# Four graph stages on one core: weight scatters placed after all gathers instead of between them

## What is computed

```python
agg = segment_sum(h[src], dst, N) / max(deg, 1); h = agg @ Wl.T + bl + h @ Wr.T      # stages 0, 1
agg = segment_sum(h[src] * norm, dst, N); h = relu(agg + b) @ W_lin + b_lin          # stages 2, 3, 4
for l in range(3):                                                                   # stages 5 to 13
    for k in (1, 2, 3):
        x = segment_sum(w * x[src], dst, N); out = out + x @ W[l, k]
    h = relu(layernorm(h + out) * gamma + beta)
```

## Time and profile before

| | us |
|---|---|
| median of 3 runs | 8722.26 |
| lowest and highest | 8720.23, 8753.76 |
| profiled execution | 8723.8 |
| its span | 8721.9 |
| stages 1, 2, 3, 4 | 561, 423, 500, 501 |
| each weighted stage | 512 to 521 |

### The profile page before, as it was taken

How to read it: one execution, slowest core, us unless ns; L and a number is a source line. 1 busy time by engine, 2 the same in 40 slices (tenths; PEclk the granted TensorE clock), 3 DMA queues, 4 the chain that set the end, 5 groups by cost and what they waited for, 6 DMA issues and landing times.

```text
span 8721.9 us, 78855 instructions
## 1 busy us (share of the span) xinstructions
PE 6499.0 (75%) x26962; PEld 3819.1 (44%) x27153; DVE 2176.5 (25%) x8462; ACT 317.1 (4%) x856; POOL 4717.8 (54%) x4964
## 2 busy tenths in 40 slices
PE   0000069698867788887898888899888888888888
PEld 0000069345444444443554444455444444544444
DVE  8220034612212211111221113222121221212233
ACT  0000000000000000000000000000000000000000
POOL 3766710124554566564656656566565656656565
PEclk9999999899988898898998999899999999999998
DMA  9047000365546555554676666667666766666765
GB/s 361 5 182 294 0 0 0 92 193 161 155 117 206 170 182 156 158 180 163 241 252 234 242 232 248 230 241 244 244 245 239 253 235 231 242 234 243 247 249 208
DMA packets 582922, 1703.65 MB, mean 195 GB/s; under 512 B 163978, under 2 KB 326211, under 8 KB 480136
## 3 DMA queue, kind: packets, MB, share of 16 engines
q1 hardware_dynamic: 317434, 1337.93, 43.4%
q0 software_dynamic: 157744, 240.14, 9.4%
q10 hardware_dynamic: 107388, 120.98, 3.9%
HBM read 1476.48 MB, written 223.40 MB: 195 GB/s over the span
## 4 chain that ended last, share of the span: by engine, by line
PE 61%; another core or an unknown queue 17%; issue 15%; DVE 3%; DMA 3%; POOL 1%; DVEq 1%; ACT 1%; ACTq 0%; SPq 0%; POOLq 0%
PE pwide L1111 31%; PE pwide L1107 14%; PE pstep L1141 8%; PE pstep L961 5%; DMA counts<-lane_val,lane_idx 1%; PE pwide L1199 1%; DMA counts<-zz 1%; PE pwide L1157 0%; PE pwide L1198 0%; POOL weights L640 0%; DVEq L1502 0%; POOL ring_f L684 0%; DVE hot L1502 0%; POOL counts L640 0%
## 5 line engine op out<-in xcount | busy, mean ns | idle before, releaser
L684 POOL DMA_INDIRECT ring_f<-table,f_src x3492 | 3325.9, 952 | 2630.5 <-issue 944.3
L1111 PE MATMUL pwide<-room,acc 128*128 128x512 f32 (+1 forms) x3920 | 1871.0, 613 | 135.1 <-issue 128.7
L1111 PE MATMUL pwide<-room,hcur 128*128 128x512 f32 (+1 forms) x3136 | 1499.9, 615 | 110.5 <-issue 109.0
L1141 PEld LDWEIGHTS pstep<-hot,ring_f 128*128 128x128 f32 x7272 | 1049.8, 200 | 714.0 <-issue 640.4
L1141 PE MATMUL pstep<-hot,ring_f 128*128 128x64 f32 x7272 | 1016.7, 273 | 287.6 <-issue 264.0
L1681 DVE TENSOR_SCALAR hot<-iota,f_win,f_wgt 128x64 f32<-128x64 f32 x2916 | 718.9, 330 | 1944.4 <-remote 936.1
L1111 PEld LDWEIGHTS pwide<-room,acc 128*128 128x128 f32 x3920 | 735.8, 199 | 848.3 <-issue 802.0
L961 PE MATMUL pstep<-acc,hot 128*128 x2058 | 445.4, 349 | 833.0 <-issue 528.9
L1107 PE MATMUL pwide<-room 128*128 128x512 bf16 (+1 forms) x2652 | 989.1, 378 | 69.8 <-issue 65.5
L640 POOL DMA_INDIRECT counts<-lane_val,lane_idx x725 | 702.3, 969 | 401.2 <-issue 253.4
L1111 PEld LDWEIGHTS pwide<-room,hcur 128*128 128x128 f32 x3136 | 588.2, 199 | 681.7 <-issue 644.0
(11 more groups left out here) (316 smaller groups left out, 2482.4 us busy)
## 6 DMA issues: line engine op xcount, KB each, us to landing
room<-weights SPq DMA_DIRECT2D x700, 1024.0 KB
room<-counts SPq DMA_DIRECT2D x600, 512.0 KB
room<-weights SPq DMA_DIRECT2D x156, 768.0 KB
weights<-zz SPq DMA_DIRECT2D x56, 1792.0 KB
counts<-zz ACTq DMA_DIRECT2D x44, 1568.0 KB
ring_f<-table,f_src POOLq DMA_INDIRECT x3492
room<-weights SPq DMA_DIRECT2D x56, 512.0 KB
table<-acc ACTq DMA_DIRECT2D x56, 256.0 KB
```

The source lines that it names most:

```text
L684: pool.indirect_dma_start(out=ring_f[:, slot, :], out_offset=None, in_=rows_from[:, :], in_offset=bass.IndirectOffsetOnAxis(ap=f_src[:, c: ...
L1111: ins = pe.matmul(bank[:, 0:w * P], x_of(a)[:, first + o, :], room[:, n % SLOTS, o * w * P:(o + 1) * w * P], start=begins, stop=ends)
L1141: ins = pe.matmul(bank[:, low:low + WIN], row, one, start=begins, stop=ends and not own, skip_group_check=True)
```

## The change

POOL no longer puts scatters between gathers. In each of stages 1 to 4 it issues all 144 gathers and then all of the stage's scatters. The edge batches are packed closer: `trail` goes from 8 to 85 in EARLY (stages 2 to 4) and from 8 to 55 in SECOND (stage 1), so the last batch stands at beat 95 instead of 170 (stage 1: 124). FIRST and LATE stay. The number of gathers, scatters, windows and matmuls is the same.

```diff
-EARLY = Split([4, 4], [4] * 10 + [1], 12, 8)
+EARLY = Split([4, 4], [4] * 10 + [1], 12, 85)
 LATE = Split([4, 4, 4, 4, 2], [4] * 7 + [3], 9, -2)
-SECOND = Split([4, 4], [4] * 10 + [1], 12, 8, FAR)
+SECOND = Split([4, 4], [4] * 10 + [1], 12, 55, FAR)
...
-WINDOW = 40
...
-                    put = 0
                     for c in range(p.pairs * CHP):
...
                         pool.indirect_dma_start(out=ring_f[:, slot, :], out_offset=None, in_=rows_from[:, :],
                                                 in_offset=bass.IndirectOffsetOnAxis(ap=f_src[:, c:c + 1], axis=0)
                                                 ).then_inc(chunk_in[slot], 16)
-                        while 0 < a < STAGES and put * p.pairs * CHP < (c + 1) * (QUOTA[a] - WINDOW):
-                            scatter(NC, sum(QUOTA[:a]) + put)
-                            put += 1
-                    while 0 < a < STAGES and put < QUOTA[a]:
-                        scatter(NC, sum(QUOTA[:a]) + put)
-                        put += 1
+                    for i in range(sum(QUOTA[:a]), sum(QUOTA[:a + 1]) if a < STAGES else 0):
+                        scatter(NC, i)
```

## The result

| | before | after |
|---|---|---|
| median, us | 8733.96 (4 runs) | 9044.47 (4 runs) |
| lowest and highest | 8720.23, 8753.76 | 9036.20, 9053.68 |
| profiled execution, its span | 8723.8, 8721.9 | 9050.08, 9048.3 |
| stages 1, 2, 3, 4 | 561, 423, 500, 501 | 621, 479, 608, 608 |
| weighted stages, from the start of stage 5 to the last matmul of a sweep | 4650 | 4641 |

What follows compares the result with a forecast made beforehand. TensorE was taken to pace stages 1 to 4, crawling beside POOL's unbroken DMA runs. Stage changes of +98, +28, +85 and +85 us summed to +296, giving 9018 us, with a range of 8850 to 9150.

Steps and rivals of the forecast that it cites:

- crawl-is-short rival: Scatter runs of stages 1 to 4: TensorE slows only in the first 40 us or at stage end; 8564 us, chance 0.08.
- the one without a crawl: Scatter tails of stages 1 to 4: POOL's DMAs do not slow TensorE at all; 8412 us, chance 0.03.
- gathers' part: Stages 1 to 4 until the last packed gather is issued: 345, 229, 237 and 238 us.
- run: All scatters of a stage unbroken after its last gather, 1.265 us each: 192 us, in stage 2 101.
- rest: Sweep left after the scatters, POOL silent, TensorE at full rate: 122, 121, 156 and 156 us in stages 1 to 4.
- The saturated half: Packed gathers make long DMA runs themselves, taking 272 us in stages 2 to 4; 9130 up to 9180 us, chance 0.12.
- 7 us of lower clock: After each stage's scatters: 7 us added because the clock stays at half for some time.
- What is moved without a price: DVE's posts, the second sparse group, the next stage's gathers and SP's wait at stage 5: shifted at no cost.
- far ahead of that: Scatters end near beat 102, well before the next stage's gathers, queued behind them on POOL, can start; no cost.

## Why the prediction was right, and where its sizes were off

**The law held, as an average.** "From about 12 us into an unbroken run of POOL's DMAs, until it ends, TensorE does 0.36 matmuls a us": measured from there on were 0.40, 0.68, 0.36 and 0.34 in stages 1 to 4. Stage 2 is nearly double, by the bursts behind late hand-offs. The 12 us don't hold for every run: in stage 6 of before, TensorE does 75 matmuls in the first 24 us of an unbroken run of 30 gathers (from 4588 us on) and crawls only then, with 5 in the next 12:

```profile
4612.00:4624.00 12.00, 2.71 (x5) 1.33 (x5) 0.00 (x0) 0.00 (x0) 9.26 (x10) 0.60 0.44 142
```

(The step of a tile in the degree walk, which the law was taken from, is 117.8 us by its own starts, not 117.6; nothing hangs on it.) The doubtful part was that it should hold for 192 us, since on the sweep no run over 55 us had been seen, and the degree walk was the only long one. It does. The crawl-is-short rival (8564) and the one without a crawl (8412) fell with it on that chip.

**The pieces of each stage**, predicted and measured, in us; "run" goes from the last gathers to the last scatter:

| stage | gathers' part | run | rest | sum |
|---|---|---|---|---|
| 1 | 345, 286 | 192, 195 | 122, 140 | 659, 621 |
| 2 | 229, 232 | 101, 112 | 121, 135 | 451, 479 |
| 3 | 237, 233 | 192, 195 | 156, 180 | 585, 608 |
| 4 | 238, 230 | 192, 195 | 156, 183 | 586, 608 |

*Gathers' part.* Right within 8 us in stages 2 to 4. In stage 1 it was 59 us too long: I took the mean of 2.89 us a beat of the old stage, and that mean held the short crawls which the interleaved scatters cause. A beat without them took 286/116 = 2.47 us. In stages 3 and 4 the same mean happened to fit; I take it that gathers packed twice as close make short stops of TensorE of their own, which was not tested. The saturated half (9130) is thereby refuted.

*Run.* The term of 1.265 us a scatter was right; with the last two gathers that join it a run of 152 is 195 us. In stage 2 the last eight gathers joined the 80 scatters: 88 issues, 112.0 us.

*Rest.* 14 to 27 us too short in each stage, and here the step failed that let TensorE go on as soon as the run ends. In stage 3 it stood until 3612.90, 18 us after the run's end, in stage 4 until 4211.23, 10 us after it, and in stage 1 from 2520.1 to 2569.96, 22 us beyond the run's end at 2547.9; in stage 2 the crawl itself goes on for 10 us. The price of what follows the run was no term of the sum, but for 7 us of lower clock. This covers roughly the whole error in stages 1 and 2, and leaves 6 us in stage 3 and 17 in stage 4 without an explanation.

That the total came so close is in part luck: the errors by stage are -38, +28, +23 and +22 us, together +35, so 296 became 331. Without the 59 us that stage 1's gathers were given too much, the sum would have been 94 us short.

**What is moved without a price.** Right on the first chip. On the second it was wrong for stage 1, and for SP's wait at stage 5, which leaves TensorE waiting 22.3 us in before and 18.6 in after. In stage 1, "far ahead of that" took TensorE's slowness for granted. The run there covers its 195 us of sweep at full rate, ends 55 us into stage 2, and holds that stage's gathers back.

**The rule on instruction fetch.** The Trainium skill, Runtime: NRT & Kernel Launch, Instruction fetch mechanics, says that engines stream their instructions autonomously and that this is mostly hidden. I used it for a rival in which TensorE isn't slowed by POOL, 8412 us. What I drew from it fails on the first chip, with 0.36 matmuls a us, and holds on the second, with 5.7. The rule itself isn't refuted: the view of the DMA queues shows only two packets of instructions in the 183 us of stage 3's slow window of after, 8 KB each, beside 65 pairs of weight load and matmul, so TensorE doesn't wait for a fetch at each pair. On the second chip the change doesn't win all the same, since the waits for POOL's order take its place.

**What stays open.** What makes TensorE crawl. Shown is that it needs indirect DMAs of POOL in close succession, that POOL's being busy isn't enough, that it isn't the DMA engines' bandwidth (share 0.06), that it isn't a fetch of instructions at each pair, that work handed to ACT and DVE starts late as well (ACT's copy in stage 3 84 us after its last matmul; DVE's post in stage 2 at 3023.79, 36 us after the products that it reads), and that one chip does it and another not, with the same program. Whether pauses or the mean rate of issues decide is open, and every edit on the first chip is a single run, which a spread of 34 us between runs of before has to be held against. Whether the second chip differs in itself or in what else ran on it, no run here tells.

## What to carry to other kernels

Where a trace shows an engine with "issue" gaps and no semaphore, look at what the other engines do in the same microseconds, take the rate beside a short run and beside a long one, and price a moved block by its unbroken length: here 152 scatters cost 186 to 196 us in one piece, and 76 of them in groups of eight with pauses of 2 to 18 us cost 5 to 31 us a stage. Place a long run on a queue so that it ends before the next stage's first instruction on that queue at the full rate of the other engines, not at the slow rate seen today. And compare versions only on one chip: the same kernel took 8744 us on one and 6722 on another, and a change that cost 3.6% where before took 8734 us cost 0.6% on the second.

## What the runs showed of the hardware

- Beside an unbroken run of indirect DMAs from POOL, on one chip TensorE started one matmul in 2.8 us, with standstills (39 us in before from 2542 us on, 34 in stage 2 of after) and a few bursts between, and its granted clock went to 0.51; the steps of POOL itself stayed at 1.265 us.
- On that chip ACT's copy of TensorE's sums came 84 us after the last matmul in stage 3 and 36 us after in stage 2, and 10 to 21 us after the run's end in stages 1, 3 and 4.
- On the other chip 152 such DMAs left TensorE 1090 matmuls in 192 us at clock 1.00, and the weighted stages took 423 to 442 us instead of 510 to 532. No weighted stage holds a scatter: the crawl stands beside runs of gathers there (5 matmuls in 12 us from 4612 us on, at clock 0.60). That it makes up the whole difference isn't shown.
- Most of the 2000 us between the two chips lies in stretches with POOL's DMAs: the sweep of stage 0 begins at 808 us instead of 1581, and nine weighted stages are some 85 us shorter each.
